# Value products of two key chunks made together every second step, over a ring of three steps of exponentials

## The reference, cut to what matters

```python
q = layernorm(q, ln_g, ln_b)
k = layernorm(k, ln_g, ln_b)
q = q * SCALE
attn = jnp.einsum('bhqd,bhkd->bhqk', q, k)
attn = jax.nn.softmax(attn, axis=-1)
out = jnp.einsum('bhqk,bhkd->bhqd', attn, v)
```

## Time and profile before

| | us |
|---|---|
| median of three runs | 6867.51 (6865.7 to 6872.63) |
| the profiled execution | 6864.03 |
| its span, first to last instruction | 6862.2 |
| TensorE busy | 6307.0 (92%) |
| VectorE busy | 3514.3 (51%) |
| ScalarE busy | 3263.7 (48%) |
| GpSimd busy | 2408.1 (35%) |
| mean granted clock of TensorE | 0.975 |

### The profile page before, as it was taken

How to read it: one execution, slowest core, us unless ns; L and a number is a source line. 1 busy time by engine, 2 the same in 40 slices (tenths; PEclk the granted TensorE clock), 3 DMA queues, 4 the chain that set the end, 5 groups by cost and what they waited for, 6 DMA issues and landing times. The chain is left out here.

```text
span 6862.2 us, 93027 instructions
## 1 busy us (share of the span) xinstructions
PE 6307.0 (92%) x35933; PEld 3091.1 (45%) x35933; DVE 3514.3 (51%) x6804; ACT 3263.7 (48%) x6001; POOL 2408.1 (35%) x2689
## 2 busy tenths in 40 slices
PE   3799999999999999999999999966999999999999
PEld 1223333333333333333333333226888888666666
DVE  3565665665656656656656566516666666000000
ACT  1366666666666666666666666522222222111111
POOL 4226436346355264363463552342222222000000
PEclk9799999999999999999999999968999999999999
DMA  2442332432432423314324324003444444311110
GB/s 64 77 76 57 67 76 56 73 69 63 76 71 55 84 57 66 78 55 73 69 63 76 70 53 75 6 16 135 157 167 154 158 162 163 121 56 56 49 56 31
DMA packets 364938, 546.09 MB, mean 80 GB/s; under 512 B 59824, under 2 KB 281984, under 8 KB 364240
## 3 DMA queue, kind: packets, MB, share of 16 engines
q1 hardware_dynamic: 321232, 498.18, 30.0%
q10 hardware_dynamic: 43264, 41.95, 1.8%
HBM read 387.94 MB, written 151.28 MB: 79 GB/s over the span
## 5 line engine op out<-in xcount | busy, mean ns | idle before, releaser
L1193 DVE TENSOR_REDUCE mx<-psum 128x1 f32<-128x401 f32 x4096 | 2212.9, 570 | 1615.7 <-PE psum L767 1606.6
L1038 ACT ACTIVATE probs<-psum 128x512 f32<-128x512 f32 (+1 forms) x3328 | 1910.6, 599 | 910.4 <-PE psum L789 907.3
L767 PE MATMUL psum<-kst,qst 96*128 96x401 bf16 x4096 | 1356.6, 343 | 192.5 <-DVE mx L1193 149.6
L789 PE MATMUL psum<-qst,kst 99*128 99x512 bf16 (+1 forms) x3328 | 1286.0, 387 | 49.9 <-ACT probs L1038 44.8
L800 PE MATMUL psum<-probs,vaug 128*17 128x512 f32 x6656 | 886.8, 605 | 0.0
L789 PEld LDWEIGHTS psum<-qst,kst 99*128 99x128 bf16 (+1 forms) x3328 | 328.8, 99 | 1178.5 <-ACT probs L1038 748.9
L767 PEld LDWEIGHTS psum<-kst,qst 96*128 96x128 bf16 x4096 | 402.7, 98 | 962.8 <-DVE mx L1193 756.3
L1460 POOL TENSOR_TENSOR disp<-disp,rz 128x2048 f32<-128x2048 f32 x64 | 294.7, 4605 | 905.5 <-DVE rz L1679 905.5
L1479 PE MATMUL psum<-phi,xT 128*128 128x128 f32 x4096 | 511.0, 279 | 39.1 <-DMA xT<-xnT_scratch 31.8
L1630 ACT ACTIVATE disp<-psum 128x512 f32<-128x512 f32 x256 | 152.8, 597 | 807.6 <-PE psum L1547 807.6
L1479 PEld LDWEIGHTS psum<-phi,xT 128*128 128x128 f32 x4096 | 479.0, 193 | 86.8 <-issue 79.1
(11 more groups left out here) (197 smaller groups left out, 7556.2 us busy)
## 6 DMA issues: line engine op xcount, KB each, us to landing
xnb<-xn_scratch SPq DMA_DIRECT2D x256, 512.0 KB, 3.6
kst<-k_planes SPq DMA_DIRECT2D x384, 200.1 KB, 8.8
k_planes<-pl SPq DMA_DIRECT2D x96, 384.0 KB, 3.2
y_scratch<-ysb ACTq DMA_DIRECT2D x128, 256.0 KB, 3.3
disp<-y_scratch SPq DMA_DIRECT2D x16, 2048.0 KB, 9.2
vaug<-v_scratch SPq DMA_DIRECT2D x64, 442.0 KB, 4.6
v_scratch<-vst SPq DMA_DIRECT2D x48, 544.0 KB, 3.1
cin<-in_ctx SPq DMA_DIRECT2D x48, 512.0 KB, 3.8
```

Source lines behind the costliest of these rows:

```text
L767: mm(to[:, 0:PW], qst[g][0:NP, j, t * P:(t + 1) * P], kst[g][0:NP, j, k0:k0 + PW], start=True, stop=True).then_inc(m_full, 1)
L789: mm(bank[S_BANK[n % 2]][0:m, :], kst[g][0:NR, j, c * P:c * P + m], qst[g][0:NR, j, :], start=True, stop=True).then_inc(s_full, 1)
L1038: fn(probs[0:m, 4 * (k % 2) + j, :], bank[S_BANK[j % 2]][0:m, :], ACT.Exp, scale=float(HD) ** 0.5).then_inc(s_exp, 1)
L1193: v.tensor_reduce(mx[:, n % 2, u // 4, u % 4:u % 4 + 1], bank[M_BANK[r % 2]][:, 0:PW], AX.X, ALU.max).then_inc(m_free, 1)
```

## The change

Three edits go together. The ring of exponentials grows from two steps to three (`probs` from 8 to 12 slots of 512), and the wait of the first exponential of step k goes from the value products of step k-2 to those of step k-3. The value products are made in steps 2, 4, ... 12 of a group for the two chunks before; the last chunk of a group is made alone in step 0 of the next group, as before. To make room, the queries of the second attention (`q1T`) lie in the fourth slot of the FFN's hidden buffer `hx`.

```diff
-        probs = sb("probs", [P, 8, S])
+        probs = sb("probs", [P, 12, S])
...
-        q1T = sb("q1T", [A1, S])
+        q1T = hx[0:A1, 3, :]
...
                 for j in range(HG):
                     last = mm(bank[V_BANK][32 * j:32 * j + HV, :], vaug[0:m, g % 2, c, HV * j:HV * (j + 1)],
-                              probs[0:m, 4 * (k % 2) + j, :], start=(c == 0), stop=(c == KC - 1), skip_group_check=True)
+                              probs[0:m, 4 * (k % 3) + j, :], start=(c == 0), stop=(c == KC - 1), skip_group_check=True)
...
-                    if c >= 1:
+                    if c >= 2 and c % 2 == 0:
+                        weigh_values(n, c - 2)
                         weigh_values(n, c - 1)
-                    elif n >= 1:
+                    elif c == 0 and n >= 1:
                         weigh_values(n - 1, KC - 1)
...
-                if j == 0 and k >= 2:
-                    act.wait_ge(pv_mm, k - 1)
-                fn(probs[0:m, 4 * (k % 2) + j, :], bank[S_BANK[j % 2]][0:m, :], ACT.Exp,
+                if j == 0 and k >= 3:
+                    act.wait_ge(pv_mm, k - 2)
+                fn(probs[0:m, 4 * (k % 3) + j, :], bank[S_BANK[j % 2]][0:m, :], ACT.Exp,
```

More of the change, by code:

```diff
@@ L468, in _ @@
             for j in range(4):
-                loads.append((probs[32 * j:32 * j + A1, :, :].rearrange("p a b -> p (a b)").rearrange(
+                loads.append((probs[32 * j:32 * j + A1, 0:8, :].rearrange("p a b -> p (a b)").rearrange(
                     "p (h n) -> p h n", h=H), w["L1_xattn_Wout"].rearrange("(h p) n -> p h n", p=A1)))
@@ L1144, in _ @@
                 setup(v.tensor_reduce(wst[32 * j:32 * j + A1, 0:D],
-                                      probs[32 * j:32 * j + A1, :, :].rearrange("p a b -> p (a b)").rearrange(
+                                      probs[32 * j:32 * j + A1, 0:8, :].rearrange("p a b -> p (a b)").rearrange(
                                           "p (h n) -> p n h", h=H), AX.X, ALU.add))
```

## The result

The changed kernel takes 6978.29 us (median of 4 runs, 6975.52 to 6982.82) against 6866.6 us for the kernel before on the same chip: ratio 1.0161, 95% interval 1.0145 to 1.0177. It is 112 us slower, where 66 were forecast. That is outside the forecast case (6905 to 6960) and inside the wider range of 6890 to 6985, 7 us from its end.

The account below looks back on a forecast made before the run. TensorE, nearly always busy in the attention loop, bounds the kernel, with value products covering other engines' bank emptying. Against 73 us of switches won stand 139 us of waits: 6864 + 66 = 6930 us; 8-in-10 range 6890 to 6985.

Parts of the forecast that it names:

- forecast case: Whole kernel: slower, at 6905 to 6960 us, chance 60%.
- layer-one queries, short planes: Two odd steps: exponential starts some 0.2 us before the value products; losses 0.34 and, averaged over rows, 0.24 us.
- residuals: One odd step: VectorE is behind with the residuals, a later 0.26 us is recovered; loss 0.62 us.
- no lag: Two odd steps per batch row where no engine lags: full 0.19 us won at each, 0.39 together.
- maxima-bound: Eight odd steps where VectorE's maxima set the time: 0.07 to 0.12 us won at each, 0.77 together.
- The switch: TensorE entering and leaving value products: 0.09 + 0.10 = 0.19 us each time, 384 saved, 73 us in all.
- rival 3: Loop: more TensorE clock drops, one to three per batch row, adding 16 to 79 us: 6950 to 7013; chance 15%.
- The 0.80: Per batch row, taken off the loss: time regained after even steps, where the odd step begins with VectorE behind.
- The switches decide: Loop: evacuations slip out from under odd-step ends, so saved switches win: 30 us faster, 6837; chance 8%.
- Half is recovered later: Loop: waits replace later ones, leaving 70 of 139 us: no change, 6865; chance 5%, up to +30 another 10%.
- The clock: The same as rival 3: more TensorE clock drops in the loop, 6950 to 7013 us, chance 15%.
- The change doesn't do what it says: Joined value products: a gap of 0.19 us between the two chunks adds 73 us, to 7007; chance 2%.

Follow-up runs that it names:

- e1: Kernel before with only the three-step ring, its looser wait and the query tile in the FFN buffer; value products in every step: 6871.64 us, ratio 0.9999.
- e2: Changed kernel with value products joined only at the ten odd steps where no engine was found late: 6857.07 us, 0.9973 of the kernel before.
- e3: Changed kernel with value products joined only at the other fourteen odd steps, where an engine was late: 7011.74 us, 1.0201 of the kernel before.
- e9: Ring of three, fourteen joined pairs chosen by the freed-banks rule at odd and even steps: 6845.98 us, 0.9954 of the kernel before.
- e10: Ring of three, thirteen joined pairs chosen by that rule, sparing the last step of each group: 6835.05 us, 0.9950 of the kernel before.
- e4: Changed kernel plus one unread product in step 31 and one in step 44 of each batch row: 6988.08 us, 1.0169 of the kernel before.
- e8: Changed kernel plus two unread products in step 31 and two in step 44 of each batch row: 7009.74 us.
- e6: Ring of three, value products in every step, ScalarE's woven evacuations one exponential later: 6980.38 us, 1.0161 of the kernel before.
- e5: Changed kernel with ScalarE's woven evacuations one exponential later in its queue: 7077.7 us, 1.0304 of the kernel before.

## Why the prediction was right or wrong

**Right: the direction and its mechanism.** The pairs, in us, as forecast in the walk through one batch row and as measured in the changed kernel. The forecast fixes the steps by the rows that it cites for 1, 7, 9, 27, 33, 35 and 44; the other step numbers I put to its kinds here.

| place | forecast | measured |
|---|---|---|
| keys' evacuation (1, 20) | +0.71, +0.71 | +0.68, +0.68 |
| queries' evacuation (7) | +0.86 | +0.56 |
| transposed x and FFN (9) | +0.88 | +0.86 |
| GpSimd's x (27) | +0.73 | +0.75 |
| layer-one exponentials (35, 37) | +0.46, +0.52 | +0.43, +0.49 |
| layer-one queries, short planes (29, 31) | +0.34, +0.24 | +0.30, +1.15 |
| residuals (44), with 46 | +0.62 | +1.15 |
| tanh queue (14) | +0.10 | +0.22 |
| three small ones (16, 42; 46 stands with 44) | +0.12 | +0.05 |
| no lag (11, 40) | -0.20, -0.20 | -0.36, +0.27 |
| maxima-bound (3, 5, 18, 22, 24, 33, 48, 50) | -0.77 | -0.88 |

Seven of the thirteen places that were forecast one by one lie within 0.05 us of the forecast. e1 shows that nothing but the order of the value products matters. e2 and e3 show that the places keep their values apart from each other, and e9 and e10 that the rule picks steps which no run had tried: nine of ten came out as wins, if one counts the one at 38, which wins in the median only.

**Wrong about the place at 40.** I had it among those without lag. The trace of the changed kernel shows the lag: the transposes of the heads (L779), which stand at the beginning of step 41, use the two banks of the row pieces, and without the cover they wait for a maximum.

```profile
1786.59 0.34 PE L767 MATMUL psum<-kst,qst 96*128 96x401 bf16 x1
1786.76 0.60 PE L779 MATMUL psum<-ident,o_sb 128*128 128x128 f32 x4
```

```profile
1821.22 0.33 PE L767 MATMUL psum<-kst,qst 96*128 96x401 bf16 x1
1821.83 0.66 PE L779 MATMUL psum<-ident,o_sb 128*128 128x128 f32 x4 [0.28 <-DVE mx L1194]
```

From piece to transposes it is 0.17 us before (first fence) and 0.61 in the changed kernel. That 0.44 turns the forecast -0.20 into +0.24, against +0.27 measured. The same wait stands in steps 15 and 28 of every row; it is the row of 12.8 us in the list of waits above.

**The switch.** 0.09 on the way in stands. The way out is not 0.10 but 0.13: one chunk holds TensorE for 0.98 to 0.99 us and two for 1.84, so 0.86 is one chunk's own work. A pair wins 0.22 instead of 0.19.

**Wrong in size: the sum per batch row.** Forecast 4.3 us, measured 6.9 (batch rows 1 to 14, 269.6 to 276.5 us). The step that failed is rival 3, which I kept out of the sum as if the clock cost nothing more: the clock drops twice in every row. Rows of the kept traces that differ in their drops alone tell most of its price:

- Steps 44 to 47 take 17.10 us before and 18.25 in the changed kernel, with 3.4 us of low clock. In e3, which joins 44 and 46 too, five rows have no drop and take 17.68. So the lag costs 0.58, near the forecast's 0.62, and the clock 0.57.
- Steps 31 and 32 take 8.30 us before without a drop and 9.88 with one, 9.2 on average, and 10.86 in the changed kernel. At full clock they would take 8.86: an estimate, the 9.72 of e4 less one added product of 0.86, if the first one costs as much as the second. (It does in batch row 15, at full clock with and without it, 8.21 and 9.07 us.) That is 0.56 for the lag, which the forecast had at 0.58 in half of the rows and 0.24 on average, and 2.0 for the clock, 1.1 more than before.

Together the clock costs some 1.7 us more per row than before, 23 us in fourteen rows, or 0.2 us per us of low clock. Were the first added product at 31 free, it would be 0.8 us per row and 11 us. In the kernel before, where rows with one drop of 3.4 us take 270.1 to 270.3 us and those without 268.7, it was 0.45: in the changed kernel part of a drop falls where TensorE would have waited anyway. At 45 it lengthens the pair at 44 by 1.55 us (from e3's +0.56 to +2.11) and shortens the one at 46 by 0.97. Of the 2.6 us above the forecast the clock is thus some 1.7, the place at 40 0.5, the one at 31 at full clock 0.3 and the one at 14 0.1. The 0.80 that I had taken off for what even steps give back did come: the places that came out below the table, 7 and 11 above all, add up to about that.

So the direction was forecast by the mechanism that the runs show. The measured +112 lies outside the +40 to +95 that the places' values gave. The wider range holds it by 7 us, and nothing in the forecast says why that range ends where it does, so that the time fell inside is partly luck.

**The rivals.** "The switches decide" fell: the kernel is slower, and 13 of the 24 pairs lose. "Half is recovered later" fell: by the pairs the waits of the lagging places stay. "The clock" came true in part: 6978 lies in its 6950 to 7013 and the drops are there, but their 11 to 23 us are less than the 84 us of switches saved (384 x 0.22), so without the lags the kernel would have been faster. "The change doesn't do what it says" fell: no gap between the chunks.

**Not settled.** What keeps the clock up at step 31: a second added product did not do it (e8), and another order of ScalarE with value products in every step nearly did (e6, one of fourteen rows with a drop) and was slower all the same. What the first added product at 31 costs in batch rows 1 to 14, and with it where in 11 to 23 us the clock's share lies: at 44 the first one cost only 0.16 (17.68 to 17.84 us without a drop). What costs at 7 besides the place in ScalarE's queue (e5).

## What to carry to other kernels

A block of work on the busiest engine can be the time in which the others empty its banks. Before moving it, ask at that place which evacuation holds the next bank and until when: if it ends later than the engine would arrive, the block gives nothing where it goes away and costs its full length where it arrives. Two neighbours are to be judged together, and a choice per place (0.995) beat the uniform rule (1.016).

## What the runs showed of the hardware

The granted clock of TensorE fell to half, 1.2 GHz, in stretches of 3.4 and 6.8 us, in the same two steps (31 and 45) of every batch row from 1 to 14: 143 us in the changed kernel, 27 before, 58 with one unread product added at two places. Ahead of the stretch at 31 TensorE had made eight products of a single column, ahead of the one at 45 it had waited 0.68 and 0.84 us within 3 us. A drop of 3.4 us cost 1.6 us at step 31 of the kernel before, and 0.57 us at step 45 of the changed kernel, where later waits became shorter by it. Added work that nobody reads cost 10 us of the 27 us that it takes.

Going from products over the full width to products in four column groups and back cost TensorE 0.09 us on the way in and 0.13 on the way out.
